# The Relu attention pass over the context: loops written out, mask added on the vector engine, scores in halves, two buffers of keys and split context

## The reference

```python
# L1_xattn: x is the normed input (128 x 256), context is 12544 x 256
q = relu(x @ W.T + b)
k = relu(context @ W.T + b)             # serves as keys and as values
s = q @ k.T                             # 128 x 12544
s = where(mask, -1e30 or lower, s)      # masked rows of the context get no weight
x = x + softmax(s) @ k
```

## Time and profile before

| | |
|---|---|
| median of 3 runs (lowest to highest) | 1556.08 us (1555.84 to 1556.17) |
| the profiled execution, its time | 1554.04 us |
| its span, first to last instruction | 1552.3 us |
| `stage_context` | 0 to 1170.5 us |
| `stage_band` and `stage_mix0` | 1170.5 to 1240.9 us |
| `stage_relu_context` | 1240.9 to 1443.0 us |
| `stage_scan` and `stage_mix1` | 1443.0 to 1552.3 us |
| busy in the span: PE, PEld, DVE, ACT, POOL | 94%, 81%, 70%, 53%, 39% |

### The profile page before, as it was taken

How to read it: one execution, slowest core, us unless ns; L and a number is a source line. 1 busy time by engine, 2 the same in 40 slices (tenths; PEclk the granted TensorE clock), 3 DMA queues, 4 the chain that set the end, 5 groups by cost and what they waited for, 6 DMA issues and landing times. The chain is left out here.

```text
span 1552.3 us, 24869 instructions
## 1 busy us (share of the span) xinstructions
PE 1461.3 (94%) x9105; PEld 1258.2 (81%) x9105; DVE 1080.9 (70%) x2053; ACT 828.1 (53%) x1578; POOL 604.7 (39%) x519
## 2 busy tenths in 40 slices
PE   6999999999999999999999999999977889999379
PEld 5888888888888888888888888888865778888248
DVE  6777777777777777777777777777775356666764
ACT  2655665556665565665565666565651255555121
POOL 6343433434343434343434343433300256665330
PEclk9999999999999999999999999999997899999779
DMA  5000000000000000000000000000007112220600
GB/s 183 1 8 18 1 25 1 25 1 25 1 25 1 25 1 25 1 24 1 24 1 24 1 24 1 1 1 1 1 28 312 63 70 71 71 71 24 284 1 4
DMA packets 9102, 57.18 MB, mean 37 GB/s; under 512 B 2121, under 2 KB 2720, under 8 KB 7969
## 3 DMA queue, kind: packets, MB, share of 16 engines
q1 hardware_dynamic: 8992, 55.73, 9.6%
HBM read 55.60 MB, written 0.13 MB: 36 GB/s over the span
## 5 line engine op out<-in xcount | busy, mean ns | idle before, releaser
L468 DVE TENSOR_TENSOR pT<-ps,pT 128x896 fp32r<-128x896 f32 x224 | 244.5, 1092 | 204.2 <-ACT pT L378 204.2
L305 POOL CAST V<-Vraw 128x512 fp32r<-128x512 f32 x189 | 115.8, 613 | 653.1 <-ACT Vraw L384 552.3
L378 ACT ACTIVATE pT<-ps 128x896 fp32r<-128x896 f32 x224 | 206.1, 920 | 179.1 <-PE ps L540 178.3
L384 ACT COPY Vraw<-ps 128x512 f32<-128x512 f32 x189 | 111.0, 587 | 265.3 <-PE ps L522 265.3
L306 POOL TENSOR_TENSOR V<-Vraw,V 128x512 fp32r<-128x512 f32 x189 | 242.3, 1282 | 15.1
L422 DVE TENSOR_REDUCE nmx<-ps 128x1 f32<-128x896 f32 x224 | 242.0, 1080 | 0.0
L365 ACT ACTIVATE prob<-ps,nm 128x896 f32<-128x896 f32 x224 | 224.2, 1001 | 0.0
L598 PE MATMUL ps<-ident,prob 128*128 128x128 f32 x1568 | 214.5, 277 | 8.6 <-ACT prob L365 4.5
L553 PEld LDWEIGHTS ps<-pT,V 128*128 128x128 f32 x1568 | 215.0, 188 | 8.3 <-issue 0.3
L553 PE MATMUL ps<-pT,V 128*128 128x256 f32 x1568 | 220.2, 280 | 0.0
L598 PEld LDWEIGHTS ps<-ident,prob 128*128 128x128 f32 x1568 | 167.5, 140 | 17.1 <-ACT prob L365 9.2
(11 more groups left out here) (307 smaller groups left out, 2398.6 us busy)
## 6 DMA issues: line engine op xcount, KB each, us to landing
raw<-in_ctxT SPq DMA_DIRECT2D x14, 896.0 KB, 4.5
d_raw<-in_ctxT SPq DMA_DIRECT2D x14, 896.0 KB, 4.6
w<-in_w SPq DMA_DIRECT2D x2, 4096.0 KB, 18.3
wg<-in_wg SPq DMA_DIRECT2D x1, 4352.0 KB, 27.5
wu<-in_wu SPq DMA_DIRECT2D x1, 4352.0 KB, 16.8
wd<-in_wd SPq DMA_DIRECT2D x1, 4352.0 KB, 26.7
e_ea<-in_alog SPq DMA_DIRECT2D x1, 2048.0 KB, 7.3
wq<-in_wq SPq DMA_DIRECT2D x1, 1024.0 KB, 5.3
```

Of the source, the lines that this page charges most:

```text
L305: link(pool, nc.gpsimd.tensor_copy(v_high(g, i), by_head(Vraw[:, j % 2, :])), "pool_chain")
L378: nc.scalar.activation(pT[u % 2][:, :, 0, :], pT_ps, ACT.Copy).then_inc(sem("pTh_ready"), 1)
L468: nc.vector.tensor_tensor(pT[u % 2][:, :, 1, :], pT_ps, pT[u % 2][:, :, 0, :].bitcast(F32), ALU.subtract).then_inc(sem("pTl_ready"), 1)
```

## The change

All of it is in `stage_relu_context` and in what feeds it.

1. The loop is gone: all 14 rounds are written out on every engine.
2. The mask row is loaded into all 128 partitions as bytes. The two mask matmuls and the bf16 row of DVE are gone. Instead DVE writes `Sm` = mask times -1e30 plus `S` to SBUF (128 x 896, one scalar_tensor_tensor from PSUM) before it takes the maximum, and the maximum and `prob` read `Sm`.
3. The scores go half by half: the matmuls with high keys of the first half wait for the third `kTh` alone, those of the second half for the fourth; then the low keys in the same way.
4. `kT`, `cTh` and `cTl` have two buffers each. The splits of chunk c+2 stay where they were in round c, but chunk 2's are made ahead of round 0, after those of chunk 1, and round 0 has none.
5. `du_free` starts from 1. `prob` of chunk c+1 waits for `du_free` to be c+2, the weighted sum of chunk c for c+1.
6. `wg` shares SBUF with the stage's buffers and is loaded at the start of `stage_scan`, between `alog` and `wu`.

The diff, cut to its core:

```diff
@@ build
-            v["wg"] = sb("wg", [P, KT, EA * F1], F32, experts)
...
+                v["d_raw"] = [sb(f"d_raw{i}", [P, KT, CK], F32, second) for i in range(2)]
+                v["d_cTh"] = [sb(f"d_cTh{i}", [P, KT, CK], F32R, second) for i in range(2)]
+                v["d_cTl"] = [sb(f"d_cTl{i}", [P, KT, CK], F32R, second) for i in range(2)]
+                v["d_kT"] = [sb(f"d_kT{i}", [P, KT, CK], F32, second) for i in range(2)]
...
+                v["early_groups"], v["early_splits"], v["early_loads"], v["groups_ahead"] = 0, 1, 1, 2 * KT
...
+            v["wg"] = sb("wg", [P, KT, EA * F1], F32, experts)
@@ stage_scan, SP
                 sp.dma_start(ea[:, :], t["alog"].partition_broadcast(P)).then_inc(sem("alog_in"), 16)
+                sp.dma_start(v["wg"][:, :, :], t["wg1"]).then_inc(sem("mix1_in"), 16)
@@ stage_relu_context, ACT
+                def exp_step(c):
+                    b = c % 2
+                    act.wait_ge(sem("dmax_done"), c + 1)
+                    act.wait_ge(sem("du_free"), c + 1)
+                    nc.scalar.activation(al[:, b:b + 1], nm[:, 1 - b:2 - b], ACT.Exp, bias=nm[:, b:b + 1], scale=-1.0)
+                    nc.scalar.activation(prob[:, :, :], Sm[:, :, :], ACT.Exp, bias=nm[:, b:b + 1], scale=1.0,
+                                         accum_out=rs[:, b:b + 1]).then_inc(sem("dexp_done"), 1)
...
+                for C in to_split[0]:
+                    split_high(C)
                 for n in range(NG):
...
                     rows_high(0, n)
...
+                for c in range(chunks):
+                    for G in range(done[c], done[c + 1]):
+                        keys(G)
+                    if c > 0:
+                        for C in to_split[c]:
+                            split_high(C)
@@ stage_relu_context, DVE
-                nc.vector.memset(one_b[:, :], 1.0).then_inc(sem("d_ones"), 1)
...
+                nc.vector.memset(nm[:, :], BIG).then_inc(sem("du_free"), 1)
...
+                    nc.vector.scalar_tensor_tensor(Sm[:, :, :], mrow[b][:, :].rearrange("p (a n) -> p a n", a=2), -BIG, S,
+                                                   ALU.mult, ALU.add).then_inc(sem("dmasked"), 1)
+                    dve.wait_ge(sem("dmasked"), c + 1)
+                    nc.vector.tensor_reduce(nmx[:, :], Sm[:, :, :], mybir.AxisListType.XY, ALU.max,
+                                            negate=True).then_inc(sem("dchunk_max"), 1)
@@ stage_relu_context, PE
                     for half, cols in enumerate(halves):
-                        nc.tensor.matmul(S[:, half, :], one_b[:, :], mneg[b][:, cols], start=True, stop=False)
...
+                        pe.wait_ge(sem("dkTh_ready"), KG * c + half + 3)
+                        for q in (qh, ql):
...
+                    for half, cols in enumerate(halves):
+                        pe.wait_ge(sem("dkTl_ready"), KG * c + half + 3)
...
+                def weighted_sum(c):
...
+                    pe.wait_ge(sem("du_free"), c + 1)
+                    pe.wait_ge(sem("dkNl_ready"), NG * (c + 1))
+                    pe.wait_ge(sem("dpTl_ready"), 2 * c + 2)
```

## The result

The changed kernel took 1561.21 us (median of 6 runs, 1560.88 to 1564.1) against 1556.2 for the kernel before: ratio 1.0036, 95% interval 1.0023 to 1.0049, so 5.0 us slower. The forecast was 1558.8, + 2.7. The profiled execution took 1560.88 us with a span of 1559.2, against 1554.04 and 1552.3. It lies 0.3 us under its median and that of before 2.2 under its own, so the two traces differ by 6.9 us where the medians differ by 5.0.

What follows compares the result with a forecast made beforehand. PE was taken to bound the kernel, with its 1.35 us a round given back to a closed chain through ACT, PE and DVE. 1.4 + 0.1 + 1.2 = + 2.7 us made 1558.8 us, range 1555.0 to 1563.5.

Steps and rivals of the forecast that it cites:

- What bounds the kernel: Steady rounds of `stage_relu_context`: PE is the bound at 13.69 us, 1.35 of it wait and mask, 12.34 without.
- The closed chain through `U`: Each steady round: `prob` waiting for the same round's `U` closes a loop through ACT, PE, DVE of 13.69 us; 78 in 100.
- Its terms: `U` to `prob` done 1.29, relu 0.69, key groups 2.72, last relu to DVE free 4.40, masked copy to `U` 4.59 us.
- PE's idle time at the third group: In each steady round PE stands still some 1.2 us ahead of the third group of keys.
- The masked copy: New DVE instruction ahead of the maximum in each round: 1.09 us, bounds 1.05 to 1.15.
- the fourth rival: POOL's split blocks the masked copy on DVE, some 1.8 us a round, 1580 us; 3 in 100.
- the second rival: Scores come late, so DVE waits for PE ahead of the masked copy, 0.3 us a round, 1563 us; 10 in 100.
- The stage's start: First rounds: ACT's extra split + 1.58, mask matmuls - 0.47, scores at low clock + 0.9; costs 1.4 us.
- The stage's end: From group three of chunk 13 to the last `U`: 18.3 us against 17.1, + 1.2 us.
- The scan's first weights: Loading `wg` at the scan's start delays `wd` some 11 us, to 1482, before first use at 1500: no cost.
- The third rival: PE's pause in each round brings the clock to 1.2 GHz for groups three and four, 2.4 us each, 1590; 3 in 100.
- The sum of + 2.7: Whole kernel: start 1.4, steady rounds 0.1, end 1.2 us, so a median of 1558.8 us.

Runs made afterwards that it cites:

- halves_alone: Kernel before with only the scores made half by half, mask matmuls and old wait kept: 1544.11 us, ratio 0.9924.
- u_before: Changed kernel, but `prob` of chunk c+1 waits for the `U` of chunk c-1 again, as in the kernel before: 1543.33 us, ratio 0.9925.
- mask_twice: Changed kernel with the masked copy made twice, the first into a buffer nobody reads: 1580.7 us, ratio 1.0154.
- u_mask_twice: u_before with the masked copy made twice, the first into a buffer nobody reads: 1545.9 us, ratio 0.9926.
- before_u_same: Kernel before with one wait moved: `prob` of chunk c+1 waits for the `U` of chunk c: 1552.68 us, ratio 0.9982.
- after_again: Changed kernel itself, unaltered, timed and profiled once more beside the kernel before: 1560.81 us, ratio 1.003.
- fill_start: Changed kernel with matmuls of no use in PE's two pauses at the stage's start: 1557.6 us, ratio 1.0010.
- u_split_fill: u_split_late with 16 matmuls of no use in PE's pause ahead of the keys of chunk 1: 1537.9 us, ratio 0.9878.
- split_late: Changed kernel with ACT's and POOL's split of the third context chunk moved back into the first round: 1558.7 us, ratio 1.0010.
- u_split_late: u_before and split_late together in one kernel: 1538.07 us, ratio 0.9880.
- fill_end: Changed kernel with matmuls of no use in PE's two pauses in the last round: 1557.2 us, ratio 1.0010.

## Why the prediction was right, and where it was off

- **What bounds the kernel: right.** PE, with 1.35 us a round that is not needed. halves_alone takes 0.73 of them, and u_before, with all of it taken and no closed chain, runs rounds of 12.47 where the prediction had 12.34 for PE alone. The rest are small hold-ups that the sum had at nothing, such as 0.06 us at the head of the keys.
- **The closed chain through `U`: right, and shown.** 13.69 us forecast, 13.69 measured. Its terms: 1.29 (measured 0.10 + 1.23), 0.69 (0.66), 2.72 (2.73), 4.40 (4.40), 4.59 (4.08 + 0.47), together 13.67 in the round shown. Opening it gives 1.22 us a round back (u_before), and a second masked copy on DVE costs 0.98 with it closed and 0.06 with it open (mask_twice, u_mask_twice). That before and after agree to a hundredth is chance: they have different bounds, as before_u_same shows, where the same wait did not lengthen the round.
- **PE's idle time at the third group: 1.2 forecast, 0.88 by the profile's count, 1.04 from start to start.** The last pair of group two starts at 1303.12 and the third group at 1304.57, 1.45 us later, where a pair takes 0.41. The first pair behind the pause then takes 0.1 longer. POOL's split (1310.49 + 4.05) costs the round's keys next to nothing: their first pair takes 0.47 us (1314.70 to 1315.17) and 0.41 in the kernel before.
- **The masked copy: 1.09 forecast, 1.08 measured,** beside POOL's split, so the fourth rival is out. The maximum from SBUF is 1.09 as assumed. `prob` from SBUF: 1.03 us, 1.02 from PSUM before, where the sum had 0.04 more.
- **The scores, the second rival: in time.** Their last matmul ends at 1311.26 and DVE comes to the masked copy at 1311.70, with no wait; only in rounds 0 and 12, where ACT has no split, does DVE stand still ahead of the copy (1.01 and 0.39 us). The casts on DVE and the low keys on POOL do hold each other up: a cast that starts beside a low key ends 0.25 us after it, and the next low key starts 0.08 us after the cast, so POOL stands still for 0.33 us. The Trainium skill, SBUF — State Buffer, "SBUF: two separate sides", has the shared port pair as an exclusive lock for a whole instruction; the trace agrees, and the margin was enough.
- **The stage's start: 1.4 forecast, 2.8 in the first profile and 1.4 in after_again (29.15 against 27.76).** In the first, up to the third group of chunk 1 the sum was right (1262.7 forecast, 1262.64). Then the masked copy came 8.03 us after it and not 6.6: PE had stood still for 2.06 us, and the clock fell a second time; in after_again, where it did not, the copy came 6.80 us after the third group. The sum held one low stretch of the clock, and allowed for that one to end earlier or later, but for none that a new pause may make. With the clock at 2.4 GHz throughout, the start takes 27.6 us with the early split (fill_start) and 25.8 without it (u_split_fill; its other wait has no part in this, since split_late and u_split_late both take 27.2): the split itself is 1.8 us, for which the sum had 1.58, and the low stretches are 1.6 to 2.9. That the first `U` came as forecast in after_again is in part luck, since the same pause let the clock fall in one profile and not in the other.
- **The stage's end: 1.2 forecast, 3.7 measured, 3.1 in after_again.** From the third group of chunk 13 the terms were 6.79 (6.6), 4.55 (4.59), 1.48 to turned `prob` (1.36), then 7.95 from turned `prob` to the end of `U` where I carried over 5.81 from the earlier trace rows. That row is of a PE that went into turned `prob` without a pause; here it had stood still for 2.51 us, and the 2.1 us are the weighted sum at 1.2 GHz. The clock fell there in both profiles, and fill_end gives 1.5 to 2.1 us of it back. It is the term that was mis-sized. The pause of 1.63 us ahead of the weighted sum stands in the kernel before too, and in u_before, and the clock stayed up in both; what is new is the one of 2.51 us.
- **The scan's first weights: 0 forecast;** the stages behind the last `U` are 0.4 us longer in the trace. The profiled executions spread by 3.9 us there, so this can't be told from nothing.
- **The third rival, the clock,** had 3 in 100 as a thing of each round, argued from windows with pauses. It stayed out of the rounds and came at the stage's edges, which I didn't look at with it. mask_twice shows how near the rounds are: one more microsecond of pause, and the clock falls in half of them.

The sum of + 2.7 stands against + 6.9 between the two traces, with the start and the end too small by 1.4 and 2.5 us. That the medians are only 5.0 us apart, because the profiled execution of the kernel before lay 2.2 us under its median, is luck for the forecast. The forecast gave even chances to within 0.2% and to slower. It came out slower; without the 2.1 us of the clock at the end it would have been 2.9, just inside.

## What to carry to other kernels

When a change moves a wait, follow it until it closes a loop: a semaphore of "the same round" instead of "the round before" joined the queues of ScalarE, TensorE and VectorE into a closed chain, in which a second masked copy of 1.08 us on VectorE cost 0.98 us a round. That wait alone was worth 1.1%. And where a change makes TensorE pause, price the matmuls behind the pause at both clocks, above all at a stage's edges, where nothing else keeps the engine busy.

## What the runs showed of the hardware that was not expected

- TensorE's granted clock fell to 1.2 GHz after single pauses of 1.81 to 2.51 us in an otherwise busy stretch, and not once in the eleven rounds with a pause of 0.82 to 0.89 us. From 1.81 to 2.06 us it did either, in the same kernel: it fell in half of the rounds of mask_twice, and in one of two profiles of the changed kernel. Matmuls of no use in the pause kept it at 2.4.
- The same code ran 6.1 us longer ahead of this stage in one execution than in another, with the granted clock at 0.71 and 0.76 instead of 0.80 and 0.84 in two stretches of 37 and 40 us.
- A VectorE cast of 128x448 took 0.39 us alone and up to 1.36 us when a GpSimd subtraction was under way, ending 0.25 us after it; the next GpSimd subtraction started 0.08 us after the cast's end. How the two interleaved was worth 0.7 us at the last cast of a round (before_u_same).
